# Half blocks on the partition halves in a selective-scan kernel: column-half sums and input products on TensorE

## The reference

```
xn = layernorm(h)
xp = xn @ x_proj_w.T              # 32 columns for dt, 16 for B, 16 for C
dt = softplus(xp[:, :32] @ dt_proj_w.T + b)
state[d, n] = exp(dt[d] * A[d, n]) * state[d, n] + dt[d] * B[n] * xn[d]      # over the 205 rows
y[d] = sum over n of state[d, n] * C[n] + D[d] * xn[d]
h = h + y
```

## Time and profile before

| | |
|---|---|
| median of 3 runs | 6246.53 us (6246.43 to 6246.85) |
| profiled execution, its own time | 6254.62 us |
| its span, first to last instruction | 6252.9 us |
| PE busy | 5809.6 us (93%) |
| POOL (GpSimd) busy | 5764.5 us (92%) |
| DVE (VectorE) busy | 5707.3 us (91%) |
| ACT (ScalarE) busy | 5106.6 us (82%) |
| mean busy share of the DMA engines (q1) | 21.8% |

### The profile page before, as it was taken

How to read it: one execution, slowest core, us unless ns; L and a number is a source line. 1 busy time by engine, 2 the same in 40 slices (tenths; PEclk the granted TensorE clock), 3 DMA queues, 4 the chain that set the end, 5 groups by cost and what they waited for, 6 DMA issues and landing times. The chain is left out here.

```text
span 6252.9 us, 111779 instructions
## 1 busy us (share of the span) xinstructions
PE 5809.6 (93%) x35091; PEld 5402.6 (86%) x35091; DVE 5707.3 (91%) x4563; ACT 5106.6 (82%) x12703; POOL 5764.5 (92%) x3740
## 2 busy tenths in 40 slices
PE   4676999999999999999999999999999999999998
PEld 3545899999999999998999999999999999999997
DVE  8776999999999999999999999999999999999995
ACT  5716888888888888888888888888888888888884
POOL 4527999999999999999999999999999999999995
PEclk9887999999999999999999999999999999999999
DMA  4601221222112221222122212221222212221220
GB/s 94 159 2 65 82 86 59 78 84 88 66 72 82 87 77 61 82 88 81 62 77 87 87 55 77 87 88 62 76 82 87 74 63 82 88 77 60 82 82 33
DMA packets 115881, 478.49 MB, mean 77 GB/s; under 512 B 17441, under 2 KB 52401, under 8 KB 107122
## 3 DMA queue, kind: packets, MB, share of 16 engines
q1 hardware_dynamic: 115314, 471.10, 21.8%
HBM read 327.82 MB, written 143.24 MB: 75 GB/s over the span
## 5 line engine op out<-in xcount | busy, mean ns | idle before, releaser
L1092 POOL TENSOR_TENSOR s_ring<-s_bc,s_u_t 128x820 f32<-128x820 f32 x2048 | 3625.0, 1789 | 3.8 <-DMA s_bc<-rows_bc 3.8
L998 ACT ACTIVATE s_decay<-s_dt_t,a_neg 128x205 f32<-128x205 f32 x8192 | 3048.0, 420 | 430.8 <-DVE s_ring L1163 358.4
L895 PE MATMUL s_y_ps<-s_ring,ident 128*128 128x205 f32 x16384 | 3157.8, 342 | 140.9 <-POOL s_ring L1098 74.5
L895 PEld LDWEIGHTS s_y_ps<-s_ring,ident 128*128 128x128 f32 x16384 | 2880.7, 192 | 232.4 <-POOL s_ring L1098 142.8
L1157 DVE TENSOR_TENSOR_SCAN s_decay<-s_decay,s_ring 128x820 f32<-128x820 f32 x1216 | 2265.2, 1863 | 216.6 <-ACT s_decay L998 214.0
L1098 POOL TENSOR_TENSOR s_ring<-s_ring,s_bc 128x820 f32<-128x820 f32 x832 | 1607.2, 1932 | 56.8 <-DVE s_ring L1157 56.6
L1157 DVE TENSOR_TENSOR_SCAN s_ring<-s_decay,s_ring 128x820 f32<-128x820 f32 x832 | 1544.2, 1856 | 45.6 <-ACT s_decay L998 43.6
L928 PE MATMUL s_xch<-s_x_t,w_low 128*128 128x205 f32 x8192 | 1524.7, 338 | 0.5 <-ACT s_x_t L1038 0.2
L928 PEld LDWEIGHTS s_xch<-s_x_t,w_low 128*128 128x128 f32 x8192 | 1423.6, 190 | 34.0 <-issue 30.5
L1163 DVE TENSOR_TENSOR s_ring<-s_decay,s_bc 128x820 f32<-128x820 f32 x1216 | 1230.3, 1012 | 41.8
L1038 ACT ACTIVATE s_x_t<-s_xch 128x512 f32<-128x512 f32 (+1 forms) x512 | 245.2, 504 | 92.6 <-PE s_xch L919 92.1
(11 more groups left out here) (163 smaller groups left out, 4377.0 us busy)
## 6 DMA issues: line engine op xcount, KB each, us to landing
s_bc<-rows_bc SPq DMA_DIRECT2D x64, 3280.0 KB, 11.1
mixed<-t_res SPq DMA_DIRECT2D x32, 1024.0 KB, 9.1
s_x_in<-mixed SPq DMA_DIRECT2D x64, 512.0 KB
s_h<-mixed SPq DMA_DIRECT2D x64, 512.0 KB
before<-s_h SPq DMA_DIRECT2D x64, 512.0 KB
out<-s_h SPq DMA_DIRECT2D x64, 512.0 KB
s_x_in<-in_txt SPq DMA_DIRECT2D x64, 308.0 KB
s_h<-in_txt SPq DMA_DIRECT2D x64, 308.0 KB
```

Source lines behind the costliest of these rows:

```text
L895: last = nc.tensor.matmul(y_ps, ident[:, :], ring[:, c % RING, n * LEN:(n + 1) * LEN], start=False, stop=(c % 4 == 3 and n == CN - 1))
L998: last = A.activation(decay[s % 2][:, n * LEN:(n + 1) * LEN], dt_t[:, par, j, :], ACT.Exp, scale=t["a_neg"][:, j, n0 + n:n0 + n + 1])
L1092: nc.gpsimd.tensor_tensor(ring[:, s % RING, :].rearrange("p (n l) -> p n l", n=CN), bc[:, par, n0:n0 + CN, :], u_t[:, j, :].unsqueeze(1).b ...
```

## The change

A chunk is now a *half block*: 64 channels with 8 states. The lower 64 partitions hold the even states and the upper 64 the odd ones, so that a chunk has again 4 x 205 elements per partition (`NB` = 16 half blocks, `NK` = 8 states per partition). Chunks s and s + 1 of a pair are the two half blocks of one block with the same states. From this follow:

- `sums` sums even and odd states and the four states per partition at once: a weight of two stacked 64 x 64 identities (`stack`) turns 128 partitions into 64 outputs. Chunk c writes the lower and chunk c + 1 the upper half of `y_ps`, their matmuls alternating. The sums come in even slots, four slots behind the scan.
- B and C arrive on each partition half with half their rows, in two transfers.
- dt and u are made for 128 channels as before (`dt_n`) and then copied by transfers of 64 partitions to both halves: four transfers per block, 32 per item for dt and 20 for u. SyncE's order is the list `SP_ORDER`.
- The first dt of each row (1e37) is written once before the loop; the copies leave it alone, and the resets go.
- For blocks 0, 2 and 4 (`ON_PE`, 12 of 32 chunks) the inputs B * u are made on TensorE (`input_products`): rows of u (transposed, `u_rows`) are the weights, and a diagonal matrix with B's values (`b_diag`, made on VectorE by `diagonals`) is what moves, in 64 x 64 pieces. They go to the PSUM buffer, and the decays of these chunks to the ring. It is done one slot ahead.
- `ON_DVE` has 13 chunks instead of 19, and all plans and `X_ORDER` have new slots.

```diff
+NB, NK = 2 * ND, NS // 2
+ON_PE = (0, 2, 4)
+AHEAD = 1
+UT = {"ut": (0, 2), "ut_hi": (4,)}
-ON_DVE = (1, 3, 4, 5, 7, 9, 11, 13, 14, 15, 17, 19, 21, 23, 24, 25, 27, 29, 31)
+ON_DVE = (0, 1, 2, 9, 10, 15, 17, 21, 22, 25, 26, 29, 30)
+SUM_LAG = LAG + 1
+SUM_SLOT = SUM_LAG % 2
-PE_PLAN = {1: [("ffn_late", 4)], 2: [("add", 0), ("add", 1)], 6: [("add", 2), ("ffn_late", 5)], 7: [("out_low", 0)],
...
+PE_PLAN = {0: [("ffn_late", 4)], 2: [("ut_hi", 0)], 3: [("add", 0)], 4: [("add", 1)], 6: [("ffn_late", 5), ("add", 2)],
+           7: [("out_low", 0)], 8: [("add", 3)], 9: [("turn1", 0)], 10: [("turn1", 1), ("turn1", 2)],
+           13: [("turn1", 3), ("ffn_late", 6)], 14: [("out_low", 1), ("xproj", (0, 4))], 17: [("xproj", (4, 8))],
+           18: [("rows", 0)], 19: [("ffn_late", 7)], 20: [("turn2", 0), ("dt", 0)], 22: [("out_high", 0)],
+           23: [("turn2", 1), ("turn2", 2)], 24: [("turn2", 3)], 25: [("out_high", 1), ("ffn", 0)], 26: [("dt", 1)],
+           27: [("ffn", 1)], 28: [("dt", 2), ("ffn", 2)], 29: [("dt", 3), ("ffn", 3), ("ut", 0)]}
...
+DVE_PLAN = {3: [("add", 0)], 4: [("add", 1)], 6: [("add", 2)], 8: [("out_low", 0)], 9: [("add", 3)], 16: [("out_low", 1)],
+            19: [("diag", 0)], 21: [("out_high", 0)], 23: [("out_high", 1)], 24: [("dt", 0)], 26: [("dt", 1)], 28: [("dt", 2)],
+            30: [("dt", 3)]}
+POOL_PLAN = {5: [("u_hi", 2)], 8: [("u_hi", 3), ("root1", 0)], 21: [("root2", 0)], 28: [("u_lo", 0)], 30: [("u_lo", 1)]}
+SP_ORDER = [("u_hi", 2), ("u_hi", 3), ("load", 0), ("spread", 0), ("keep", 0), ("steps", 0), ("u_lo", 0), ("steps", 1),
+            ("steps", 2), ("write", 0), ("load_rows", 0), ("steps", 3), ("u_lo", 1)]
...
+            def halves(target, place, j, first, signal):
+                for i in range(2):
+                    for h in range(2):
+                        sp.dma_start(target[64 * i:64 * i + 64, place + h, first:],
+                                     dt_n[64 * h:64 * h + 64, j, first:]).then_inc(signal, 16)
...
             def sums(u, par, c):
-                for n in range(CN):
-                    last = nc.tensor.matmul(y_ps, ident[:, :], ring[:, c % RING, n * LEN:(n + 1) * LEN],
-                                            start=False, stop=(c % 4 == 3 and n == CN - 1))
-                last.then_inc(sum_done, 1)
+                for n in range(CN):
+                    for h in range(2):
+                        last = nc.tensor.matmul(y_ps[sides[h], :], t["stack"][:, :], ring[:, (c + h) % RING, n * LEN:(n + 1) * LEN],
+                                                start=False, stop=(c % 4 == 2 and n == CN - 1))
+                        if n == CN - 1:
+                            last.then_inc(sum_done, 1)
+
+            def input_products(u, par, s, x):
+                j, k0, bank = s // 4, CN * (s // 2 % 2), s % 2
+                before = (s - 2) % CHUNKS
+                if before in ON_DVE:
+                    wait(pe, dve_hc, u * PER_DVE + by_dve(before) if s >= 2 else (u - 1) * PER_DVE + by_dve(before))
+                else:
+                    wait(pe, scan_done, u * CHUNKS + s - 1)
+                if s % 4 == 0:
+                    wait(pe, p_empty, u * P_USES + 2)
+                    emptied(x, "ut" if j in UT["ut"] else "ut_hi")
+                out = decay[bank].rearrange("p (k l) -> p k l", k=CN)
+                for turn in range(2):
+                    if turn:
+                        wait(pe, half_made, (u * MADE_ON_PE + made_on_pe(s)) * 4)
+                    for g in (1, 0):
+                        for r in (1, 0):
+                            l0 = 128 * g + 64 * r
+                            w = min(64, LEN - l0)
+                            half, rows_r = turn ^ r, slice(64 * r, 64 * r + w)
+                            for i in range(2):
+                                n0 = 2 * (k0 + 2 * half) + i
+                                last = nc.tensor.matmul(
+                                    out[64 * i:64 * i + 64, 2 * half:2 * half + 2, l0:l0 + w],
+                                    u_rows[rows_r, g, P * UT_PLACE[j] + 64 * (s % 2):P * UT_PLACE[j] + 64 * (s % 2) + 64],
+                                    b_diag[rows_r, g, n0:n0 + 3:2, 0:w], start=True, stop=True)
+                                if g == 0 and turn == 0:
+                                    last.then_inc(half_made, 1)
+                last.then_inc(made_by_pe, 1)
...
+            def turn_u(name, v, x):
+                bank, full = claim(x, name, 0)
+                wait(pe, u_done, v * 4 + max(UT[name]) // 2 + 1)
...
-                if s % 16 == 0:
-                    wait(act, reset_done, u * 2 + s // 16 + 1)
+                target = ring[:, s % RING, :] if from_pe else decay[s % 2]
...
             def scaled_input(v, par, r, x):
-                wait(pool, p_empty, v * P_USES + r + 2)
+                wait(pool, dt_in[r], v * DT_COPIES + DT_COPIES)
...
+            def diagonals(v, par, r, x):
+                for g, n in ((0, P), (1, LEN - P)):
+                    last = V.tensor_tensor(b_diag[0:n, g, :, :], t["stack"][0:n, :].unsqueeze(1).broadcast_to([n, NS, 64]),
+                                           p_ps[0:n, P * g + RANK + 1:P * g + RANK + 1 + NS].unsqueeze(2).broadcast_to([n, NS, 64]), ALU.mult)
```

More of the change, by code:

```diff
@@ L43 @@
 CW = CN * LEN
-CHUNKS = ND * NS // CN
+CHUNKS = NB * NK // CN
 LN_EXP_TABLES = 6
@@ new lines, in inputs @@
+            def inputs(v, r):
+                wait(sp, u_done, v * 4 + r + 1)
+                for j in (2 * r, 2 * r + 1):
+                    if j not in ON_PE:
+                        halves(u_t, 2 * U_PLACE[j], j, 0, u_in[r])
+            def entry(u, par, x, groups, ahead=True):
+                for name, arg in SP_ORDER:
+                    if name == "keep" and "add" in groups:
+                        keep(u - 1, 1 - par, x)
+                    if name == "load" and "turn1" in groups and ahead:
+                        load(u + 2, x)
+                    if name == "spread" and "turn1" in groups:
+                        spread(u + 1, 1 - par)
+                    if name == "write" and "out_low" in groups:
+                        write(u - 2, par, x)
+                    if name == "load_rows" and (not isinstance(u, int) or 0 <= u < BATCH):
+                        load_rows(u, par)
+                    if name == "steps" and "turn1" in groups:
+                        steps(u + 1, 1 - par, arg)
+                    if name == "u_lo" and "turn1" in groups:
+                        inputs(u + 1, arg)
+                    if name == "u_hi" and (not isinstance(u, int) or 0 <= u < BATCH):
+                        inputs(u, arg)
```

272 lines of the change are left out of this document (168 added, 104 removed), and 8 rows, old and new, of the table ACT_PLAN.

## The result

| | median | range of the runs |
|---|---|---|
| before | 6246.7 us | 6246.4 to 6250.0 |
| after | 6940.7 us | 6926.3 to 6944.2 |

The ratio is 1.110 [1.109, 1.112]: the change makes the kernel 694 us slower. The forecast was 5990 us.

What follows compares the result with a forecast made beforehand. POOL was taken as fullest, 86.6 of 88.16 us per item. DVE's 79.4 plus waits of 3.7 and 1.0 gave 84.1; saving 4.06 x 63 = 256 us gave 5990 us, range 5790 to 6250.

Steps and rivals of the forecast that it cites:

- their sums: Work per item after the change: POOL 76.7, DVE 79.4, ACT 77.2 us.
- column halves share: PE's sums: instructions alternating between column halves run side by side, taking 22.3 us per item instead of 44.5.
- Rival D: PE's sums: column halves don't share for float32 on 128 rows; up to +22.3 us, period 106, 7390 us; chance 0.03.
- its smaller form: PE's sums: weights in the open, 0.05 us for each of 128 instructions; +6.8 us, period 90.9, 6420 us; within chance 0.03.
- 1.0 us for slots 20 to 31: Late half: POOL's input of chunk 31 ready at 35.8 us, DVE arrives at 35.0; 1.0 us taken with a chunk 28 wait.
- rival E: Late half: u_lo 1 waits for SP's copies, then transposes of u and sums wait; +3 us, period 87.2, 6190 us; chance 0.16.
- My own test: Sign that the forecast is wrong: POOL waits for s_dt_n by more than 2 us an item.
- 1.25 + 0.09: PE's input products: a chunk occupies 1.25 us, 15.0 for 12; each change of shape between jobs costs 0.09 us.
- the sum has 3.7: Blocks 0, 2 and 4, made on PE: DVE's waits for PE together 3.7 us per item.
- rival C: PE's products: small matmuls don't overlap, 2.2 us a chunk; period 95.5, 6710 us; decides from 1.6 us; chance 0.09.
- The 0.06 us for the semaphore: Wait between a chunk's two turns on PE: 0.06 us, beside 0.16 from last column to matmul end.
- A: The forecast itself: PE's products in time but not free; period 82.5 to 86.5 us, 5855 to 6140 us; chance 0.52.

Runs made afterwards that it cites:

- again_beside: Changed kernel with the 13-row pair computed twice per turn, the second right behind the first, no added change of shape: 7150.7 us, 1.144.
- again_apart: Changed kernel with the 13-row pair computed twice per turn, the second behind the first 64-row pair, four more changes of shape per chunk: 7997.8 us, 1.281.
- wide_products: Changed kernel with input products as 128-row matmuls (zeros behind row 77 of the second group), 8 instead of 16 per chunk, no wait between turns: 6720.9 us, 1.076.
- the mended kernel: Changed kernel with dt copies merged and issued earlier, 128-row products, late ffn 4 moved, and 30 items per loop turn: 6248.1 us, 1.000.
- the tail: Changed kernel with dt copies of two blocks in four transfers instead of eight, and steps 1 issued ahead of u_lo 0: 6598.4 us, 1.057.
- the one attempt on the second: The 30-items-per-turn kernel with all edits, plus second half of the projection, rows, diagonals and dt 0 each moved one slot later: 6526.5 us, 1.045.

## Why the prediction was wrong, step by step

**Right.** What three of the engines would do: POOL, DVE and ACT came within 0.5 us of their sums. (That POOL bound the kernel before fits its 98% in the earlier trace rows; no run tests it alone.) That column halves share: in the trace after, the two instructions of a pair of sums start 7 ns apart and the next pair 0.17 us later, so 16 instructions occupy 1.49 to 1.54 us. The forecast had 1.39, and had priced the change to the next work apart, at 0.09. Rival D with its 0.174 from each to the next is refuted, also in its smaller form, which would have added 0.4 us to every 16. The rule of the Trainium skill that was weighed there (TensorE: Matmul & The Clock Gate, The mechanism), that a weight load overlaps only matmuls of another row group, isn't borne out: every instruction of the sums uses all rows, and the pairs follow each other at 0.17 us all the same. The diagonals (two of 1.2 us per item) and DMA (31.2% of the queue, where I had 25% and said that twice as much would be hidden) were no trouble.

**The first failed step is the late half of the item.** The forecast's sum has 1.0 us for slots 20 to 31; slots 28 to 31 alone stood 8.2 us over DVE's work. What was mis-sized is the chain that the prediction knew as rival E. The mechanism stands in the prediction in the right order (copies behind others on SyncE, u_lo 1, the transposes of u, the sums behind them), at +3 us per item and a chance of 0.16. It measured 5.4 us per item (342 / 63), as one chain, and it was not an alternative to the forecast's terms but came on top. Two things were wrong. The issue of a copy from partition to partition was 0.63 us, not 0.44 from a row of another kind of transfer, so eight took 5.0 and not 3.5; and I let the chain end at PE's sums. It goes on into the next item, by ACT's copy of u's rows, and the sums at its end ran at the lower clock level. My own test for it was in the text: POOL waiting over 2 us for the copies; it waits 7.0.

**The second is the price of a chunk of products,** 1.79 us and not 1.25 + 0.09; the blocks that hold them stood 9.3 us over DVE's work, where the sum has 3.7. The price is above 1.6, the point from which rival C decides, and C had 0.09. I had summed the columns of the busiest tile (4 x 0.109 us), which puts the 13-row pair at nothing, and charged changes of shape only where PE goes from one kind of work to another. Both failed inside the chunk: per turn the pair takes 0.12 us of its own and the change from 13 to 64 rows 0.13 (again_beside and again_apart), 0.49 us for two turns. I had read 0.09 for another pair of shapes. The Trainium skill (TensorEngine Tiling (Array Packing), Key Properties) has the rule that I had weighed for the changes between jobs; I did not put it to the pieces within one. C's mechanism, small matmuls that don't overlap, was the wrong one: they do, since parting the column halves cost some 0.6 us per chunk. The 0.06 us for the semaphore in the same sum has no row behind it; with the 0.16 beside it the trace shows 0.26. What the price did to the period is seen in wide_products: -3.5 us per item.

**The third is missing altogether:** the jump of the loop. It cost 1.8 us in the kernel before and 5.9 in the changed one, and in the mended one 6.5 as the mean of the 28 that were taken away. The forecast took the period as equal for all items.

**Together.** Of the 694 us, 342 went with the tail, 168 more with wide pieces and a later ffn, 182 more with 28 jumps fewer; that is 692, and the kernel is level with before. That isn't quite a comparison of the same things, since the kernel before gains 49 us by 30 items to a turn, too. The forecast's gain of 256 us is not in the mended kernel either. There PE is busy 84.4 us per item (845.61 x 88.07/882), where the forecast had 82.5 and a period 1.6 above; the period is 3.6 above. DVE stands idle longest in slots 4 to 7 (2.1 us, where the late ffn now is) and 16 to 19 (1.9 us); the one attempt on the second failed. Whether a better plan exists for these slots stays open.

Two numbers of the rivals don't follow from their terms, and nothing hangs on them: a period of 82.5 us gives 5890 us as the edge of A, not 5855, and D's 128 instructions at 0.05 us are 6.4 us, not 6.8.

## What to carry to other kernels

Price transfers by their count on the issuing queue, from a row of transfers of the same kind, and follow a late landing through each engine's fixed order until something has slack, into the next iteration if need be. A matmul cut into pieces that leave a remainder of another height pays for the remainder's own instructions and for each change of height. Here whole-height pieces with zeros, which also needed no wait in the middle, were 0.3 us cheaper per chunk. Count code as well as work: when a loop body grows, run it once with more iterations to a turn, before and after.
